# Softplus's "+ 1" moves from VectorE to ScalarE under one table set, and the out-projection alternates two images

## The reference, cut to what matters

```python
dts = jax.nn.softplus(dts + dt_projs_b[None, :, :, None])   # step sizes, 4 directions x 192 channels x 1024 pixels
As = -jnp.exp(A_logs).reshape(K, DI, N)                     # N = 16 states
# per step t:  dA = exp(d_t * As);  h = h * dA + d_t * u_t * B_t;  y = sum over states of h * C_t
...
y = (y - mu) / jnp.sqrt(var + 1e-05) * out_norm_g + out_norm_b
y = y * jax.nn.silu(z)
return y @ out_proj_w.T                                     # 192 -> 384 channels
```

## Time and profile before

| engine | busy us | share of the span |
|---|---|---|
| PE | 2276.9 | 82% |
| DVE | 1734.4 | 62% |
| ACT | 1189.9 | 43% |
| POOL | 1160.4 | 42% |

### The profile page before, as it was taken

How to read it: one execution, slowest core, us unless ns; L and a number is a source line. 1 busy time by engine, 2 the same in 40 slices (tenths; PEclk the granted TensorE clock), 3 DMA queues, 4 the chain that set the end, 5 groups by cost and what they waited for, 6 DMA issues and landing times.

```text
span 2787.9 us, 21841 instructions
## 1 busy us (share of the span) xinstructions
PE 2276.9 (82%) x6404; PEld 1034.7 (37%) x6404; DVE 1734.4 (62%) x1497; ACT 1189.9 (43%) x1301; POOL 1160.4 (42%) x551
## 2 busy tenths in 40 slices
PE   4887877778787777778777776889988649999998
PEld 2333323323332333333233322444455425555554
DVE  2436999999999999999999997752122200000000
ACT  1226666666676666657666664211111111111111
POOL 0002767776676777667676764000000141111111
PEclk9988999999999999999999999789999769999999
DMA  5111000000000000000000002201011252222220
GB/s 193 56 25 44 1 0 1 0 0 0 0 0 0 0 0 0 0 0 0 0 0 0 0 0 108 83 34 45 1 45 45 92 189 101 102 104 102 104 101 17
DMA packets 44296, 111.04 MB, mean 40 GB/s; under 512 B 5168, under 2 KB 30883, under 8 KB 42978
## 3 DMA queue, kind: packets, MB, share of 16 engines
q1 hardware_dynamic: 38114, 93.59, 9.5%
q0 software_dynamic: 6144, 16.98, 1.7%
HBM read 74.68 MB, written 34.67 MB: 39 GB/s over the span
## 4 chain that ended last, share of the span: by engine, by line
PE 47%; issue 22%; DVE 18%; ACT 8%; POOL 3%; DMA 1%; DVEq 1%; SPq 0%; ACTq 0%; POOLq 0%
PE ps L975 9%; PE ps L987 9%; DVE ps L1123 8%; PE ps L756 5%; ACT arena L525 3%; POOL arena L385 3%; DVE arena L1131 3%; PE ps L700 3%; PE ps L939 2%; PE ps L737 2%; PE ps L825 2%; PE ps L864 2%; PE ps L711 2%; PE ps L727 2%; ACT arena L533 2%
## 5 line engine op out<-in xcount | busy, mean ns | idle before, releaser
L385 POOL TENSOR_TENSOR arena<-arena 128x1024 f32<-128x1024 f32 x384 | 975.5, 2540 | 438.4 <-DVE arena L1131 423.5
L1131 DVE TENSOR_TENSOR_SCAN arena<-arena,ps 128x1024 f32<-128x1024 f32 x384 | 878.1, 2287 | 13.3
L756 PE MATMUL ps<-arena 128*128 128x512 f32 x1536 | 777.9, 631 | 43.0 <-DVE arena L1110 40.1
L737 PE MATMUL ps<-arena 96*128 (+1 forms) x1536 | 424.3, 395 | 275.0 <-DVE arena L1131 236.2
L533 ACT ACTIVATE arena<-ps 128x1024 f32<-128x1024 f32 x384 | 392.4, 1022 | 437.6 <-PE ps L737 435.3
L1123 DVE TENSOR_TENSOR ps<-ps,arena 128x1024 f32<-128x1024 f32 x384 | 465.9, 1213 | 35.2 <-PE ps L737 32.7
L525 ACT ACTIVATE arena<-arena 128x1024 f32<-128x1024 f32 x384 | 438.5, 1142 | 0.3
L756 PEld LDWEIGHTS ps<-arena 128*128 128x128 f32 x1536 | 309.8, 203 | 313.6 <-issue 252.0
L737 PEld LDWEIGHTS ps<-arena 96*128 96x128 bf16 x1536 | 126.5, 100 | 688.5 <-DVE arena L1131 445.5
L1344 DVE TENSOR_TENSOR arena<-ps,arena 128x384 f32<-128x384 f32 x32 | 17.9, 558 | 450.2 <-PE ps L987 450.2
L987 PE MATMUL ps<-arena 128*128 128x384 f32 x768 | 250.2, 486 | 0.0
(11 more groups left out here) (166 smaller groups left out, 1708.6 us busy)
## 6 DMA issues: line engine op xcount, KB each, us to landing
arena<-in_w SPq DMA_DIRECT2D x16, 2304.0 KB, 16.1
slot_in<-arena SPq DMA_DIRECT2D x8, 772.0 KB, 16.0
arena<-slot_in SPq DMA_DIRECT2D x8, 772.0 KB, 18.4
arena<-in_xT SPq DMA_DIRECT2D x4, 1536.0 KB, 9.3
arena<-in_x_tok SPq DMA_DIRECT2D x1, 6144.0 KB, 21.5
tokens<-arena SPq DMA_DIRECT2D x4, 1536.0 KB, 5.8
out<-arena SPq DMA_DIRECT2D x4, 1536.0 KB, 9.6
z_scratch<-arena SPq DMA_DIRECT2D x4, 768.0 KB, 5.5
```

Source lines behind the costliest of these rows:

```text
L385: nc.gpsimd.tensor_tensor(hst[:, u % RING], hst[:, u % RING], c_sb[:, u % RING], ALU.mult).then_inc(p2_ok, 1)
L737: mm = pe.matmul(dst[:, h * 512:(h + 1) * 512], sel_lhs[0:BR, n], bc[0:BR, q // J, dr, m, h * 512:(h + 1) * 512], start=True, stop=True)
L756: mm = pe.matmul(Y_PS[:, h * 512:(h + 1) * 512], ident, hst[:, u % RING, h * 512:(h + 1) * 512], start=(u == 0), stop=(u == UN - 1))
L1131: nc.vector.tensor_tensor_scan(h, f, x, 0.0, ALU.mult, ALU.add).then_inc(sc_ok, 1)
```

## The change

In the scan stage `w = u + 1` leaves DVE's stream at n = 8 and becomes an ACT instruction at n = 8 (Identity with a bias of one). A preload ahead of the scan names a table set that has both exp and ln. In the gated stage `out_proj` takes one tile index `i` for both images and alternates them matmul by matmul, into two neighbouring PSUM banks. Tiles 0 and 1 (of both images) come ahead of the means, tile 2 ahead of the sums of squares, tile 3 after them. DVE's additions and statistics follow the same order, with a settling step and two small copies per group instead of one.

```diff
-DELTA_AT = (8, 9, 11, 12)
+DELTA_AT = (9, 11, 12)
-ACT_AT = (5, 6, 7, 10)
+ACT_AT = (5, 6, 7, 8, 10)
...
+        OP_PAIR, OP_BACK, OP_SEEN = (2, 4, 6, 4), (8, 4, 8, 4), 8
+
+        def op_bank(i, r):
+            return OP_PAIR[i] + r
...
+                elif step == 3:
+
+                    act.wait_ge(u_ok, jq + 1)
+                    nc.scalar.activation(t_w, dux[:, dr], ACT.Identity, bias=ones[:, 0:1]).then_inc(w_ok, 1)
...
+            nc.scalar.preload_act_table_set("natural_log_exp_and_others")
...
-            def out_proj(c, r, tiles):
-                lo = H2 * r
-                pe.wait_ge(yg_ok, 1 + c * J + J)
-                for i in tiles:
-
-                    pe.wait_ge(ta_ok, c * 8 + (4 * r + i + 1))
-                    for j in range(J):
-                        mm = pe.matmul(ps[:, 2 + i, 0:C], yg[lo:lo + H2, j, i * P:(i + 1) * P], w_out[lo:lo + H2, j],
+            def out_proj(c, i):
+
+                if i == 0:
+                    pe.wait_ge(yg_ok, 1 + c * J + J)
+                for r in range(2):
+                    pe.wait_ge(ta_ok, c * 8 + (OP_SEEN + 2 * i + r + 1 - OP_BACK[i]))
+                for j in range(J):
+                    for r in range(2):
+                        lo, hi = H2 * r, H2 * r + H2
+                        mm = pe.matmul(ps[:, op_bank(i, r), 0:C], yg[lo:hi, j, i * P:(i + 1) * P], w_out[lo:hi, j],
                                        start=(j == 0), stop=(j == J - 1))
-                    mm.then_inc(op_ok, 1)
+                        if j == J - 1:
+                            mm.then_inc(op_ok, 1)
 
             def gated_steps(c, last):
-                out_proj(c, 0, range(2))
+                out_proj(c, 0)
+                out_proj(c, 1)
                 if not last:
                     mean_sums(c + 1)
-                out_proj(c, 0, range(2, 4))
-                out_proj(c, 1, range(1))
+                out_proj(c, 2)
                 if not last:
                     square_sums(c + 1)
-                out_proj(c, 1, range(1, 4))
+                out_proj(c, 3)
...
-                    dve.wait_ge(u_ok, jq + 1)
-                    nc.vector.tensor_scalar(t_w, dux[:, dr], 1.0, None, ALU.add).then_inc(w_ok, 1)
-                elif step == 1:
-
...
+            def add_tokens(c, tiles):
+                first = (c // 2) * (2 * TB) + (c % 2) * 4
+                lo, n = min(tiles), len(tiles)
                 for i in tiles:
-                    dve.wait_ge(op_ok, 1 + c * 8 + (4 * r + i + 1))
-                    row = tok[:, first + i, :]
-                    nc.vector.tensor_tensor(row, row, ps[:, 2 + i, 0:C], ALU.add).then_inc(ta_ok, 1)
...
+                    for r in range(2):
+                        dve.wait_ge(op_ok, 1 + c * 8 + (2 * i + r + 1))
+                        row = tok[:, first + r * TB + i, :]
+                        nc.vector.tensor_tensor(row, row, ps[:, op_bank(i, r), 0:C], ALU.add).then_inc(ta_ok, 1)
```

More of the change, by code:

```diff
@@ L312, in _ @@
                 sp.dma_start(z4, z_dram[c // 2, :, :, bass.ts(c % 2, HALF)]).then_inc(ld_z, 16)
-            sp.wait_ge(ta_ok, 4 + NT)
+            sp.wait_ge(ta_ok, OP_SEEN + NT)
             w1_v = a["w1"].rearrange("e (t p) m -> e p t m", p=P)
@@ L846, in _ @@
             pe.wait_ge(ld5, 16 * 9)
-            pe.wait_ge(ta_ok, 4 + NT)
+            pe.wait_ge(ta_ok, OP_SEEN + NT)
             def turn(b, i):
@@ L1007, in _ @@
             dve.sem_inc(sc_ok, 2)
-            dve.sem_inc(ta_ok, 4)
+            dve.sem_inc(ta_ok, OP_SEEN)
             for s in (yg_ok, ta2_ok, bd_ok, ob_ok):
@@ L1094, in delta @@
                                                    op0=ALU.add, op1=ALU.subtract).then_inc(lost_ok, 1)
-                elif step == 2:
+                elif step == 1:
                     dve.wait_ge(ln_ok, jq + 1)
@@ L1099, in delta @@
                                                    op0=ALU.max, op1=ALU.add).then_inc(pd_ok, 1)
-                elif step == 3:
+                elif step == 2:
                     dve.wait_ge(pd_ok, jq + 1)
@@ L1173, in gate_y @@
                     nc.vector.tensor_tensor(yg[:, j], yt[:, j], z4[:, j], ALU.mult).then_inc(yg_ok, 1)
-            def add_tokens(c, r, tiles):
-                first = (c // 2) * (2 * TB) + (c % 2) * 4 + r * TB
+            def add_tokens(c, tiles):
+                first = (c // 2) * (2 * TB) + (c % 2) * 4
+                lo, n = min(tiles), len(tiles)
                 for i in tiles:
-                    dve.wait_ge(op_ok, 1 + c * 8 + (4 * r + i + 1))
-                    row = tok[:, first + i, :]
-                    nc.vector.tensor_tensor(row, row, ps[:, 2 + i, 0:C], ALU.add).then_inc(ta_ok, 1)
-                dve.wait_ge(ta_ok, c * 8 + (4 + 4 * r + max(tiles) + 1))
+                    for r in range(2):
+                        dve.wait_ge(op_ok, 1 + c * 8 + (2 * i + r + 1))
+                        row = tok[:, first + r * TB + i, :]
+                        nc.vector.tensor_tensor(row, row, ps[:, op_bank(i, r), 0:C], ALU.add).then_inc(ta_ok, 1)
+                dve.wait_ge(ta_ok, c * 8 + (OP_SEEN + 2 * (lo + n)))
                 settled(dve)
                 for i in tiles:
-                    ins = nc.vector.bn_stats(tbst[:, i], tok[:, first + i, :])
+                    for r in range(2):
+                        ins = nc.vector.bn_stats(tbst[:, r * n + i - lo], tok[:, first + r * TB + i, :])
                 chain.link(ins)
                 settled(dve)
-                for i in tiles:
-                    ins = nc.vector.bn_aggr(tmv[:, i], tbst[:, i])
+                for k in range(2 * n):
+                    ins = nc.vector.bn_aggr(tmv[:, k], tbst[:, k])
                 chain.link(ins)
-                lo, hi = min(tiles), max(tiles) + 1
-                chain.link(nc.vector.tensor_copy(tstat[:, bass.ds(first + lo, hi - lo), :], tmv[:, lo:hi]))
+                settled(dve)
+                for r in range(2):
+                    ins = nc.vector.tensor_copy(tstat[:, bass.ds(first + r * TB + lo, n), :], tmv[:, r * n:r * n + n])
+                chain.link(ins)
             def gated_steps(c, last):
@@ L1196, in gated_steps @@
                     add_orders(c + 1)
-                add_tokens(c, 0, range(2))
+                add_tokens(c, range(2))
                 if not last:
                     centre(c + 1)
-                add_tokens(c, 0, range(2, 4))
-                add_tokens(c, 1, range(1))
+                add_tokens(c, range(2, 3))
                 if not last:
@@ L1204, in gated_steps @@
                     gate_y(c + 1)
-                add_tokens(c, 1, range(1, 4))
+                add_tokens(c, range(3, 4))
             add_orders(0)
@@ L1212, in _ @@
             with nc.vector.Fori(0, 2 * NP - 1) as c:
-                chain.enter(c, 13)
+                chain.enter(c, 10)
                 gated_steps(c, False)
```

## The result

Before: 2788.27 us, the median of four runs (2787.69 to 2788.8). Changed: 2756.03 us, four runs (2753.77 to 2759.09). The ratio is 0.9885, interval 0.9868 to 0.9902: the change takes 32.2 us off, where 22.8 were forecast. The profiled run took 2757.09 us with a span of 2755.3; before it was 2789.66 and 2787.9. In what follows, stages are compared by these two profiled runs, 32.6 us of span apart.

What follows compares the result with a forecast made beforehand. DVE paces the scan; a PE-DVE chain bounds the gated stage. Terms -13.3 + 0.4 - 2.0 - 1.8 - 6.1 = -22.8 us from 2789.66 give 2766.9, as median 2765.5; own range 2758 to 2773, with rivals A and B 2750 to 2781.

Steps and rivals of the forecast that it cites:

- Work off DVE: Scan stage: the addition leaves DVE, freeing 0.58 us at each of 23 places between scans, 13.3 us less.
- ACT has the room: Scan stage: the addition, at most 1.06 us, fits on ACT within its 1.13 us wait before the n = 10 copy.
- Table loads worth nothing: Scan stage: ACT loses 48 table loads, 61.6 us, worth nothing by itself since DVE doesn't wait for ACT.
- Waits after L1110: Scan stage: DVE's waits for PE after y is emptied shrink by 2 us; 17 us if all tiles matched the last.
- Rival A: Scan stage: waits after L1110 shrink to the last tile's everywhere, 15 us more gain, 2750.5 us; chance 0.12.
- Rival B: Scan stage: PE's lower clock eats the gain, at most 13.3 us, and the shorter waits, 2781 us; chance 0.08.
- The passes overlap: Gated stage, out-projection: alternated passes of both images run side by side, one step per pair, 0.32 us at full clock.
- Rivals C and D: Out-projection: C, no overlap, 2782 us, chance 0.06; D, weight loads no longer beside passes, slower, 2807 us, chance 0.04.
- Chunks that have a follower: Gated stage, three chunks followed by another: 0.6 us less each, 1.8 us in all, bounds 0 and 3 x 1.6.
- Last chunk: Gated stage: the last chunk's 48 passes take 14.9 us instead of 21.31; stage ends 6.1 us earlier, bounds 0 and 8.3.
- The opening: Ahead of the scan: the first addition takes 1.06 us on ACT for 0.67 on DVE, +0.4 us.
- Nothing behind the gated stage: Everything after the gated stage: forecast difference 0 us.

Runs made afterwards that it cites:

- dve_add_kept: The changed kernel with an addition of the same size put back on DVE at n = 8, its result unused: 2776.8 us, ratio 0.9959.

## Why the prediction came out as it did

The time was inside the range of 2750 to 2781 us, but under the forecast's own of 2758 to 2773 us: the gain was 9.5 us larger than the sum. The two main mechanisms were the ones forecast; three terms were sized wrong (the waits, the last chunk, what follows the gated stage), and one came out near by luck. Step by step:

- **Work off DVE, 23 x 0.58 = 13.3 us.** Held: DVE's busy time in the scan fell by 13.8 us and the stream by as much. Putting the addition back alone (dve_add_kept) shows the same from the other side.
- **ACT has the room.** Held; moving the addition without the preload gave the same time. The margin was as thin as said: in a middle tile of the changed kernel the copy of n = 10 starts about 0.1 us after ACT is free, where ACT waited 1.13 us for PE before; it still waits 2.44 us for DVE's L1102 behind it, and DVE waits for nobody there. The copy is the second row:

```profile
1130.93 1.16 ACT L534 ACTIVATE arena<-arena 128x1024 f32<-128x1024 f32 x1
1132.18 1.02 ACT L542 ACTIVATE arena<-ps 128x1024 f32<-128x1024 f32 x1
1135.65 1.06 ACT L521 ACTIVATE arena<-arena 128x1024 f32<-128x1024 f32 x1 [2.44 <-DVE arena L1102]
```

  The rule of the Trainium skill, ScalarE: Activation LUTs, "Rules for kernel authors", that adds belong on VectorE, holds for the instruction (1.156 against 0.669 us) and not for this kernel: the move gives about 20 us.
- **Table loads worth nothing.** Held, and shown by itself: 0.9999.
- **Waits after L1110, 2 us less.** This is the step that failed most: 8.4 us. I had bounded it by 17 us, from the last tile's row, and then sized it by the middle tiles' row, since "these are most of the tiles". But the row of a middle tile belongs to a tile of 122.9 us. With a shorter tile the clock comes back at another place, and two tiles of three wait 1.3 to 1.6 us less. dve_add_kept shows that the length decides. Rival A took the right mechanism and the wrong extent: the waits are near those of the last tile in two tiles of three, not everywhere. Rival B, that less room turns into new waits, didn't occur.
- **The passes overlap.** Held: 12 passes in 2.21 us at full clock is 0.37 per pair, near the 0.32 forecast. The 24 passes ahead of the means took 7.03, 6.67 and 6.16 us. Rivals C and D are out. On a drain: the Trainium skill, TensorEngine Tiling (Array Packing), "Key Properties", says that changing the tiling mode drains TensorE and changing only the tile doesn't. The trace has 128-row passes that start at 1763.44 and take 2.84 us; the 64-row ones behind them start at 1766.21, as the former end. No pause of a tenth of a microsecond shows at the change. So a drain isn't seen at this scale, and that a change of the tile alone doesn't drain agrees with the overlap.
- **Chunks that have a follower, 3 x 0.6 = 1.8 us.** Came out as 1.1 in sum, near the forecast by luck. From one chunk's first pass to the next's they gained 1.3, lost 0.3 and gained 0 us. Over the three, what stands behind the sums of squares took 1.5 us less, and this is the 1.8 that was forecast. But the sums also began 5.3 us sooner behind the first pass (forecast: as before) and ran 5.7 us longer (forecast: unchanged), and these two cancelled. In the second chunk the passes ahead of the means were quicker than forecast (6.67 us, not 8.6) and the means ran at full clock. Centring waited for DVE's own statistics, as forecast: it starts 0.44 us behind the copies of L1205, long after the means, and is 0.2 us late, not 1.0. What the step missed is what the faster PE did next: it ran dry 3.93 us ahead of the sums of squares, its clock fell, and they took 1.4 us longer. I had taken their 2.84 us over from the earlier trace rows unchanged. The other order of this stage bears it out: with work put into that gap, the sums run at full clock in two turns of three, which gives 4.0 of the 14 us by which that kernel is faster.
- **Last chunk, 6.1 us.** Measured 7.3. All 48 passes took 10.72 us, not 14.9: I had costed the first 18 steps with the time of 18 passes at a clock of 0.53, and in an equal stretch the clock was now 0.74 on average. Not all of that arrives, since DVE is last: its last two additions start 3.2 us after the last pass. So "DVE has the tiles 0 to 2 done about 0.3 us after" failed, and of the 10.6 us that PE's passes lost, the chunk gave 7.3.
- **The opening.** +0.6 against +0.4 in the prologue, and +1.0 us ahead of the first out-projection, where the means wait for mean_w's transfer (5.72 us, before 5.3) and run at a lower clock (5.00 us, before 4.54). The forecast had nothing there.
- **Nothing behind the gated stage.** Failed: 3.6 us. The work there is the same in all kernels. It takes 922.8 to 924.3 us in the seven that have the out-projection half, and 926.8 to 927.0 in four that don't. But in the kernel before with y emptied earlier, which doesn't have that half either, it takes 924.5 us, so the half can't be the whole cause. Of the 3.6 us, 2.4 arise in the first 120 us of this stretch, where PE's mean clock was 0.92 before and is 0.94 in the changed kernel, and 0.94 as well in the kernel before with y emptied earlier. So the lower clock falls on less of the same work. What decides that was not tested, and stays open.

Of the signs named beforehand, three were met: DVE's busy time down by about 16 us (15.9 over the run), the gated stage 5 to 12 us shorter (7.4), no table load in the scan. Two were met but for their size: the tile is 2.05 us shorter, and the last chunk's passes took 10.7, not 13 to 15.5 us.

## What to carry to other kernels

A wait that comes from the clock of TensorE has no fixed size: it depends on where in the loop the clock comes back, so when the loop's length changes, range over all its rows instead of taking the commonest. When one engine becomes faster in a chain, ask where it will idle next; start the chain's next link earlier and put independent work into the gap before tuning the order within its own work. And look for what opens the idle gap itself: moving the one instruction that TensorE waits for gave more than the change (36 against 32 us).

## What the runs showed of the hardware

- fp32 passes on 64 rows each, on the two halves of the array, overlap even when three of one half stand in order ahead of three of the other: 12 passes in 2.95 us at full clock, against 2.21 alternated and 3.84 for 12 starts 0.32 us apart.
- The scan's waits depended on the length of a tile: 32.7 us in all at a mean of 122.77 us a tile, 32.2 at 122.74, 24.3 at 120.72. Of the 2 us between the last two, 1.16 are DVE's work (two additions a tile at 0.58); the rest is the shorter waits.
- Behind an idle time of 3.65 us PE's next four passes were slow in the first ten tiles of the changed kernel that have such a gap, all ten of them (3.32 to 3.78 us, where 1.88 is full speed). Behind one of 1.34 us, with y emptied earlier, they were slow in three of ten (3.12 to 3.67 us) and took 1.98 us in the other seven. The slow ones cost nothing there, since DVE did not wait for them.
- A table load on ACT takes 1.283 us, and 48 of them were worth 0 us to a kernel that is bound elsewhere.
